# Eight-head chunk attention: from units of 256 tokens on two bank pairs to blocks of 512 tokens on four shared banks

## What is computed

```python
# layer 0 (per sample; q, k from y, v from x)
scores = q @ k.T / sqrt(256)                  # channels x channels of a head
o = Wo @ (softmax(scores) @ v) + bo + x
x1 = group_norm(o) * gn_w + gn_b              # one mean and variance over the sample
# layer 1 (per chunk of 64 tokens, per head; q, k, v from y)
scores = q @ k.T / sqrt(32) + where(mask > 0, 0, -1e9)
u = (softmax(scores) @ v) @ W_out.T + b_out
z = u * mask + x1
out = (z - mean_t(z)) / sqrt(var_t(z) + eps)  # over the tokens of a channel
```

## Time and profile before

| | |
|---|---|
| time, median of 3 runs | 1542.44 us (1541.51 to 1542.45) |
| profiled execution: time | 1542.93 us |
| profiled execution: span | 1541.1 us |
| PE busy | 1511.2 us, 98% |
| PE weight loads | 1274.8 us, 83% |
| DVE busy | 1278.6 us, 83% |
| ACT busy | 1108.9 us, 72% |
| POOL busy | 450.8 us, 29% |
| mean share of TensorE's clock granted | 0.995 |

### The profile page before, as it was taken

How to read it: one execution, slowest core, us unless ns; L and a number is a source line. 1 busy time by engine, 2 the same in 40 slices (tenths; PEclk the granted TensorE clock), 3 DMA queues, 4 the chain that set the end, 5 groups by cost and what they waited for, 6 DMA issues and landing times.

```text
span 1541.1 us, 54826 instructions
## 1 busy us (share of the span) xinstructions
PE 1511.2 (98%) x24146; PEld 1274.8 (83%) x24146; DVE 1278.6 (83%) x2024; ACT 1108.9 (72%) x2064; POOL 450.8 (29%) x294
## 2 busy tenths in 40 slices
PE   9999999999999999999999999999999999999995
PEld 6888888888888888888888888888888888888883
DVE  5778888888788887978879888888888889788897
ACT  6667676777767777677776776867767776777765
POOL 1114133141331413314142141422314133141321
PEclk9999999999999999999999999999999999999998
DMA  7232331423315233142422414233142331524212
GB/s 250 56 99 83 111 124 38 152 84 118 111 36 152 84 118 111 54 148 71 143 86 84 132 57 145 84 111 121 55 151 78 120 116 41 149 83 129 59 49 91
DMA packets 96397, 157.28 MB, mean 102 GB/s; under 512 B 5408, under 2 KB 38304, under 8 KB 96032
## 3 DMA queue, kind: packets, MB, share of 16 engines
q1 hardware_dynamic: 96160, 153.78, 31.8%
HBM read 120.20 MB, written 33.55 MB: 100 GB/s over the span
## 4 chain that ended last, share of the span: by engine, by line
PE 96%; DVE 1%; ACT 1%; issue 1%; POOL 0%; ACTq 0%; POOLq 0%; DVEq 0%
PE pj_ps L313 46%; PE l_ps L313 12%; PE s_ps L328 9%; PE w_ps L339 8%; PE l_ps L424 7%; PE w_ps L357 7%; PE l_ps L441 2%; PE l_ps L468 2%; PE l_ps L462 1%; PE l_ps L471 1%; PE s_ps L499 0%; PE l_ps L450 0%; DVE o_sb L972 0%; PE l_ps L432 0%; PE l_ps L489 0%
## 5 line engine op out<-in xcount | busy, mean ns | idle before, releaser
L1132 POOL TENSOR_TENSOR prob<-prob,row_inv 128x1024 f32<-128x1024 f32 x128 | 257.9, 2015 | 890.4 <-DVE row_inv L864 890.4
L671 ACT CAST att_hi<-w_ps 128x256 fp32r<-128x256 f32 x256 | 83.2, 380 | 192.2 <-PE w_ps L357 192.1
L313 PE MATMUL pj_ps<-y_hi,w_hi 128*128 128x512 f32 x510 | 207.4, 407 | 0.0
L313 PE MATMUL pj_ps<-y_hi,w_lo 128*128 128x512 f32 x510 | 202.0, 396 | 0.0
L313 PE MATMUL pj_ps<-y_lo,w_hi 128*128 128x512 f32 x510 | 202.0, 396 | 0.0
L859 DVE TENSOR_REDUCE row_sum<-prob 128x16 f32<-128x1024 f32 x128 | 155.0, 1211 | 49.2 <-ACT prob L640 49.1
L847 DVE TENSOR_REDUCE row_max<-s_ps 128x16 f32<-128x1024 f32 x128 | 155.6, 1215 | 21.2 <-PE s_ps L328 21.2
L328 PEld LDWEIGHTS s_ps<-k_s,q_s 32*64 32x64 f32 x8192 | 130.8, 133 | 43.1 <-issue 35.2
L1149 POOL TENSOR_TENSOR o_sb<-o_sb,u_sb 128x1024 f32<-128x1024 f32 x60 | 157.7, 2638 | 0.9
L854 DVE TENSOR_TENSOR prob<-s_ps,row_max 128x1024 f32<-128x1024 f32 x128 | 155.6, 1215 | 0.1
L635 ACT COPY prob_t<-w_ps 128x512 f32<-128x512 f32 x256 | 152.2, 596 | 3.8 <-PE w_ps L339 3.1
(11 more groups left out here) (139 smaller groups left out, 3552.2 us busy)
## 6 DMA issues: line engine op xcount, KB each, us to landing
y_raw<-in_ctx SPq DMA_DIRECT2D x64, 512.0 KB, 4.9
yt_raw<-in_ctx_t SPq DMA_DIRECT2D x64, 512.0 KB, 4.6
x_raw<-in_x SPq DMA_DIRECT2D x64, 512.0 KB, 5.1
out_z<-o_sb SPq DMA_DIRECT2D x60, 512.0 KB, 3.6
mask_b<-in_mask SPq DMA_DIRECT2D x64, 256.0 KB, 4.0
out_z<-o_sb SPq DMA_DIRECT2D x8, 256.0 KB, 2.7
u_sb<-in_w SPq DMA_DIRECT2D x2, 512.0 KB, 5.8
w_sb<-in_w SPq DMA_DIRECT2D x1, 1024.0 KB, 10.7
```

The source lines that it names most:

```text
L313: last = mm(dst, lhs, rhs, start=i == 0, stop=i == len(todo) - 1)
L1132: nc.gpsimd.tensor_tensor(cut, cut, row_inv[:, u % 2, :].unsqueeze(2).to_broadcast([P, 2 * HEADS, CHUNK]), ALU.mult).then_inc(probs_done, 1)
```

## The change

The attention goes by whole blocks of 512 tokens, and one tensor `s_ps` of four banks serves scores, transposes and values in turn; `w_ps` is gone. Head `i` of a group of four now has bank `i`. `scores` makes its 64 products of a block in one burst: four heads in turn take the four row groups and go to the same half of the columns, and the next four to the other half. `top`, `shift`, `exponents`, `sums` and `scale_probs` take two banks at a time (`e` = 0, 1), as many elements as a unit had. `transpose` turns two banks at a time, eight tiles each, and waits until `shift` has read the next block's scores out of these banks. `values` writes banks 0 and 1, in two calls for two pairs of chunks each, one before and one behind the first key projection. `copy_att` and `att_low` take 512 columns at a time where they took 256. `preset_mask` of banks 0 and 1 waits for `att_low`, that of banks 2 and 3 for the copies of the transposes. `q_s`, `k_s`, `att_hi` and `att_lo` are held once.

The order of all four bodies is written anew. PE's is shown whole below; ACT's and DVE's follow it. On ACT, the order of slot 1 of a block is the copy of the first key half, `copy_att`, the copy of the second, `preset_mask` of banks 0 and 1, `split_y`; `copy_v` follows. On DVE, slot 2 of a block has `split_y`, `branch`, then both pairs of `top` and `shift`; the mean over the sample comes in slot 0 ahead of the first Gram split, and the deviation behind the flags and the first sums. Slot 1's share of the closing result of a sample goes from DVE to ACT, its other quarters and their stores to slots 10, 13 and 14, and the closing norm's shift is held with its sign turned, so that both engines use the same. The first block's scores, maxima and exponents go ahead of the loop, and the end of the last sample is written to match. Numbers of products, transposes and elementwise elements stay the same.

```diff
--- before
+++ after
-        s_ps = es.enter_context(nc.psum_tensor("s_ps", [P, 2, 2, HALVES, 2, CHUNK], F32))
-        w_ps = es.enter_context(nc.psum_tensor("w_ps", [P, 2, 512], F32))
-        pt_ps = w_ps[:, :, :].rearrange("p j (q m) -> p j q m", q=HP)
-        av_ps = w_ps[:, :, 0:HALVES * P].rearrange("p c (g j q) -> p c g j q", g=HALVES, j=2)
+        s_ps = es.enter_context(nc.psum_tensor("s_ps", [P, HP, QUADS, HALVES, 2, CHUNK], F32))
+        pt_ps = s_ps[:, :, :, :, :, :].rearrange("p i f g c k -> p i f g (c k)")
+        av_ps = s_ps[:, 0:2].rearrange("p c f g e k -> p c (f g e k)").rearrange("p c (g j q) -> p c g j q", g=HALVES, j=PAIRS)
...
+            def scores(n, b):
+                pe.wait_ge(qkv_copied, count(n, 24, 6 * b + 3))
+                pe.wait_ge(mask_set, count(n, 8, 2 * b + 1))
+                for f in range(QUADS):
                     for g in range(HALVES):
+                        for c in range(2):
+                            for h in range(2):
+                                t = 4 * f + 2 * h + c
+                                cut = slice(t * CHUNK, (t + 1) * CHUNK)
+                                for i in range(HP):
+                                    rows = slice(DH * i, DH * i + DH)
+                                    last = mm(s_ps[64 * h:64 * h + 64, i, f, g, c, :], q_s[rows, g, cut], k_s[rows, g, cut],
+                                              start=False, stop=True, skip_group_check=True)
                 last.then_inc(scores_ready, 1)
+            def transpose(n, b, e):
+                pe.wait_ge(probs_done, count(n, 8, 2 * b + e))
+                if n == SAMPLES - 1 and b == BLOCKS - 1:
+                    pe.wait_ge(att_lo_done, count(n, 4, b - 1))
+                else:
+                    pe.wait_ge(shifted, count(n, 8, 2 * (b + 1) + e))
+                for i in (2 * e, 2 * e + 1):
+                    for f in range(QUADS):
+                        for g in range(HALVES):
+                            last = mm(pt_ps[:, i, f, g, :], prob[:, b % 2, i, f, g, :], ident, start=f == 0 and g == 0, stop=True, is_transpose=True,
+                                      skip_group_check=True)
+                    last.then_inc(transposed, 1)
+            def values(n, b, pairs=range(PAIRS)):
+                pe.wait_ge(qkv_copied, count(n, 24, 6 * b + 5))
+                pe.wait_ge(pt_copied, count(n, 16, 4 * b + 3))
+                for j in pairs:
+                    f, h = divmod(j, 2)
                     for g in range(HALVES):
                         for c in range(2):
                             rows = slice(CHUNK * c, CHUNK * c + CHUNK)
+                            for i in range(HP):
                                 o = g * P + DH * i
+                                last = mm(av_ps[DH * i:DH * i + DH, c, g, j, :], v_s[rows, b % 2, j, o:o + DH],
+                                          prob_t[rows, i, f, g, h, :], start=j == 0 and g == 0, stop=True, skip_group_check=True)
+                if pairs[-1] == PAIRS - 1:
+                    last.then_inc(av_ready, 1)
...
+                    behind = not (first and b == 0)
+                    if j == 0:
+                        if behind:
+                            transpose(n, b - 1, 0)
+                        if ahead:
+                            qk(n, b + 1, Q_W, 0)
+                        if behind:
+                            transpose(n, b - 1, 1)
+                        if s == S_MX:
+                            layer0_output(n, 0)
+                        if ahead:
+                            qk(n, b + 1, Q_W, 1)
+                        if s == S_GRAM[2]:
+                            gram_part(n, 2)
+                        if s == 0 and not first:
+                            mean_over_partitions(n - 1)
+                        if behind:
+                            values(n, b - 1, range(2))
+                        if s == 0 and not first:
+                            variance_over_partitions(n - 1)
+                        if s == S_MX:
+                            layer0_output(n, 1)
+                    elif j == 1:
+                        if ahead:
+                            qk(n, b + 1, K_W, 0)
+                        if behind:
+                            values(n, b - 1, range(2, PAIRS))
+                        if s == S_GRAM[0]:
+                            gram_part(n, 0)
+                        if ahead:
+                            qk(n, b + 1, K_W, 1)
+                        if s == S_GRAM[3]:
+                            gram_part(n, 3)
+                    elif j == 2:
+                        if ahead:
+                            v(n, b + 1, 0)
+                        if s == S_MX + 2:
+                            layer0_output(n, 2)
+                        if behind:
+                            wout(n, b - 1, 0)
+                        if s == S_GRAM[1]:
+                            gram_part(n, 1)
+                        if s == S_HLT:
+                            layer0(n, s)
+                        if ahead:
+                            scores(n, b + 1)
+                        if s == S_MX + 2:
+                            layer0_output(n, 3)
+                    else:
+                        if ahead:
+                            v(n, b + 1, 1)
+                        if s == S_SUM:
+                            layer0(n, s)
+                        if behind:
+                            wout(n, b - 1, 1)
+                    if s not in (S_HLT, S_SUM):
+                        layer0(n, s)
...
+            def copy_pt(n, b, e):
+                for i in (2 * e, 2 * e + 1):
+                    act.wait_ge(transposed, count(n, 16, 4 * b + i))
+                    copy(prob_t[:, i].rearrange("p f g h q -> p (f g h q)"), pt_ps[:, i].rearrange("p f g m -> p (f g m)")).then_inc(pt_copied, 1)
...
+                act.wait_ge(blocked_done, count(n, 4, b))
+                if not exists(n, 4, b - 1):
+                    act.wait_ge(banks_open, 1)
+                elif not exists(n, 4, b - 2):
+                    act.wait_ge(shifted, count(n, 8, u - 2))
+                elif e == 0:
+                    act.wait_ge(att_lo_done, count(n, 4, b - 2))
                 else:
+                    act.wait_ge(pt_copied, count(n, 16, 4 * (b - 2) + 3))
+                for i in (2 * e, 2 * e + 1):
+                    last = copy(pt_ps[:, i], blocked[:, b % 2].unsqueeze(2).to_broadcast([P, QUADS, HALVES, P]))
                 last.then_inc(mask_set, 1)
...
+            def copy_att(n, b):
+                act.wait_ge(av_ready, count(n, 4, b))
+                if exists(n, 8, 2 * (b - 1) + 1):
+                    act.wait_ge(wout_ready, count(n, 8, 2 * (b - 1) + 1))
                 for g in range(HALVES):
+                    last = copy(att_hi[:, g, :].rearrange("p (j c q) -> p c j q", j=PAIRS, c=2), av_ps[:, :, g, :, :])
                 last.then_inc(att_hi_done, 1)
...
+                    if j == 0:
+                        if behind:
+                            copy_pt(n, b - 1, 0)
+                        if ahead:
+                            copy_q(n, b + 1, 0)
+                        if behind:
+                            copy_pt(n, b - 1, 1)
+                        if s == S_MX:
+                            copy_output(n, 0)
+                            split_x(n, 1)
+                        if ahead:
+                            copy_q(n, b + 1, 1)
+                        if behind:
+                            exponents(n, 2 * b + 1)
+                        if s == S_GRAM[3] - 1:
+                            split_yt(n, 3)
+                        if ahead:
+                            preset_mask(n, 2 * (b + 1) + 1)
+                        if not first and s == 4:
+                            group_normed(n - 1, 1)
+                    elif j == 1:
+                        if s == S_MX + 1:
+                            copy_output(n, 1)
+                            split_x(n, 2)
+                        if ahead:
+                            copy_k(n, b + 1, 0)
+                        if behind:
+                            copy_att(n, b - 1)
+                        if s == S_GRAM[0]:
+                            split_yt(n, 1)
+                        if ahead:
+                            copy_k(n, b + 1, 1)
+                            preset_mask(n, 2 * (b + 1))
+                        if s == S_HL:
+                            copy_hl(n)
+                        if not (last and b + 2 >= BLOCKS):
+                            split_y(n, b + 2)
...
+            def att_low(n, b):
+                dve.wait_ge(att_hi_done, count(n, 4, b))
                 for g in range(HALVES):
+                    hi, lo = (a[:, g, :].rearrange("p (j c q) -> p c j q", j=PAIRS, c=2) for a in (att_hi, att_lo))
                     last = tt(lo, av_ps[:, :, g, :, :], hi, ALU.subtract)
                 last.then_inc(att_lo_done, 1)
...
```

(56 more changed lines are left out.)

445 lines of the change are left out of this document (164 added, 281 removed).

## The result

The changed kernel takes 1566.29 us (median of four, 1562.05 to 1568.82), the kernel before 1541.97 beside it: ratio 1.0156, interval 1.0138 to 1.0174. It is slower by 24 us. The profiled execution is the lowest of the four, 1562.05 us with a span of 1560.3, 19.2 us above the span before.

The account below looks back on a forecast made before the run. TensorE's own work was taken as the bound. Per sample, 0.3 us of burst gain against 3.1 us of four new waits made +2.2 us; fifteen samples plus 1 us at the way in gave 1575 us, range 1525 to 1640.

Parts of the forecast that it names:

- Second output of layer 0: Slot 12: TensorE waits for the single-buffered split of x between first and second output, 0.8 us a sample (0.7 to 0.9).
- Third output: Layer 0's third output: TensorE waits for x's low part, late behind `copy_att` and `att_low`, 1.1 us (0.8 to 1.4).
- Variance: Variance matmul ahead of the first key projection: TensorE waits for DVE's deviation, 0.6 us a sample (0 to 1.4).
- `att_low` to the next transposes: Blocks 1 and 2: ACT's and DVE's chain outlasts TensorE's filler, 0.3 us a block, 0.6 a sample.
- The score burst: One burst of 128 score products per block, priced at 1.88 us, between 2.18 and the values' pace, 1.58.
- Stalls inside the bursts: TensorE stalls within score and value bursts: no term of their own; the forecast started from a clean sample of 93.65 us.
- Sum of a sample: Per sample: 93.65 - 0.3 + 3.1 = 96.45 us against 94.26, so +2.2 us.
- Way in and ends: Before the first sample and at the tail: first exponents now ahead of first copies, 1 us (0 to 4).
- SP's queue: Moved stores ahead of SP's loads of x: costed at nothing, since loads are issued two quarters ahead of use.
- the faster one: Rival: score burst shrinks to 1.09 us and only the two waits for x remain, 1509 us; chance 0.2.
- No gain in the burst: Rival: the score burst stays at 2.18 us, 18 us over the forecast, 1593 us; within the forecast's own range.
- every hand-over in the open: Rival, slower by more: 6.2 us of waits a sample and a 2.18 us score burst, 1640 us; chance 0.2.

Follow-up runs that it names:

- e1: Changed kernel with a second buffer each for x_hi and x_lo, so splitting x waits for the output two back: 1539.1 us, ratio 0.9984 to the kernel before.
- e2: Changed kernel with the product for the variance over partitions issued behind the first key half of slot 1, not ahead of it: 1559.67 us, ratio 1.0122.
- e13: Changed kernel with score products reordered: 64 in a row on four tiles, then 64 on the other four: 1581.17 us, ratio 1.0266.
- e5: Changed kernel with block 0's exponents and the second mask preset later on ACT, and a last-sample store issued earlier: 1561.3 us, ratio 1.0127.
- e9: Changed kernel with each 128-product score burst cut in two halves around the first half of the output projection: 1586.36 us, ratio 1.0294.
- e4: Changed kernel with a block's values as one whole burst again, ahead of the first key half: 1594.55 us, ratio 1.0350.
- e11: Changed kernel with the edits of e1, e2 and e5 together and the last sample's end reordered: 1519.18 us, ratio 0.9860.

## Why the prediction was right where it was, and wrong where it was

The forecast was 1575 us, slower by 33; measured are 1566, slower by 24. The direction and the mechanism were right: TensorE was and stays the bound, and waits of the hand-overs outweigh what its bursts gain. The sizes follow by step.

- *Second output of layer 0*: 0.8 us a sample, measured 0.9. Right, and its cause shown by e1.
- *Third output*: 1.1, measured 0.8, the low end of its bounds; e1 removes it with the other, 1.76 together.
- *Variance*: 0.6, measured 0.5 to 0.6. e2 takes 0.64 off the median sample.
- *`att_low` to the next transposes*: 0.6, measured at most 0.1. The transposes of a plain sample follow at 0.79 to 0.86 us for eight, and no wait of this kind stands in the list. My low end, 0, was the case.
- *The score burst*: 1.88, measured 1.52, just under the bound from the values' pace. This is the term that was most off: PE's work fell by 1.69 us a sample and not by 0.3. I interpolated between 17.0 ns and the values' 12.3, because I had the values' pace for 64 only; e13 shows that the slow pace belongs to four tiles alone and has nothing to say about eight. It also shows 2.18 to be too much for four: 128 products in two turns of 64 take 1.93, since part of the 1.09 is paid once a burst.
- *Stalls inside the bursts*: not in the sum, which starts from the clean sample and lets today's 0.6 us of waits go without a reason. The rows of before show these stalls: 5.1 us, eight times, in the values that follow 64 scores without a break, 4.6 us of it in the fourteen samples. They did not go: the score bursts of after have 5.5 us of them there, 0.4 a sample.
- *Sum of a sample*: +2.2 forecast; -1.4 for the burst, -0.5 for the transposes, -0.3 for the third output, +0.1 for the second, +0.4 for the stalls make +0.5, and the windows say 5.26 / 14 = 0.38.
- *Way in and ends*: 1 us, 0 to 4, measured 7.95 + 4.1 + 1.9 = 14 in the profiled execution. This step failed outright. I had named one cause at the way in (exponents ahead of copies) and put it at 1 us beside work that I did not check for being there; the preset ahead of the copy of `v`, with the slow clock behind its wait, I had not seen; and at the last sample I counted the products and not the order, which lost the bursts that lay beside the chain to `m_lo`.
- *SP's queue*, costed at nothing: in the samples it was nothing. In the last one the order was the reverse of what I feared, a store behind a load, and with the wait gone in e5 the end is no shorter.

So 1575 came near 1566 in part by chance: the steady part was forecast 28 us too slow (33 against 5), the ends 13 too fast, and the other three executions lie 4 to 7 us above the profiled one. Of the rivals, the faster one had the right kind of condition, a burst under 1.55 us with both waits for `x` alone (from its own terms the limit comes to 1.65); the burst did pass it, but the variance, the stalls and the ends took the gain. *No gain in the burst* is excluded by the 1.52 us, *every hand-over in the open* by the windows and the list of waits.

What stays open: why 128 products on eight tiles take 1.52 us where four take 1.93, and not half; when TensorE asks for the next piece of its instructions; and where the rest of the way in goes.

## What to carry to other kernels

When several steps are put on the same banks, price each hand-over as the other engines' chain against TensorE's filler between the two ends: four such sums gave three waits to within 0.3 us, and one buffer more (`x` in two, 26 us) took the two largest back. Give small tiled products as many tiles of the array as the program order can keep at work, and cut runs of over a hundred of them by long products where two halves cost little more than the whole, as the values' do; for the scores of e9 the cut cost more than the stalls. Price the first and the last sample by their own order; here they held nearly three quarters of the profiled loss.

## What the runs showed of the hardware

- A burst of 128 small products takes 1.93 us with 64 in a row on four tiles (35 start in 0.5 us) and 1.52 where eight take turns (47 start); the banks that they write, two or four in turn, shared by row groups or not, changed the burst by 0.1 us at most.
- Instructions arrive in pieces of 16 KB, 191 in the run, and runs of small products stall for up to 4.2 us (e1), until 1.2 to 1.6 us after a piece has landed; in the kernels before and after and in e4 all 54 such stalls come at the same place of TensorE's instructions, counted modulo 256.
- Behind an idle stretch of 2.18 us twelve products ran at the 1.2 GHz level, 0.43 us apart; in e11, with 0.36 us of idling at the same place, the like are 0.23 apart. The level also fell behind the 1.80 us at the way in, for 6.5 us, and did not behind 2.54 us there.
